# Where the experts of a strip stand in a hand-written slot plan: five slots or three

## What is computed

```python
x = x + _L0_conv_ref(_ln_c(x), ...)      # attention over routed regions, 8 heads of 8
t = t + _L0_ffn_ref(_ln_t(t), ...)       # 8 experts of 64x64, top 2
x = x + _L1_conv_ref(_ln_c(x), kernel)   # 3x3 convolution, binarized weights
t = t + _L1_ffn_ref(_ln_t(t), ...)       # 8 experts of 64x128, top 2
```

```python
for e in range(E):
    h = gelu(tokens @ w1[e] + b1[e]); y = h @ w2[e] + b2[e]
    out = out + combine[:, e:e + 1] * y
```

## Time and profile before

| | us |
|---|---|
| median of 3 runs | 6992.14 (6990.91 to 6999.84) |
| the profiled execution's own span | 6996.9 |
| VectorE busy | 6258.5 (89%) |
| TensorE busy | 5469.8 (78%) |
| GpSimd busy | 4062.8 (58%) |
| ScalarE busy | 3507.3 (50%) |

### The profile page before, as it was taken

One profiled execution on the slowest core, in us unless ns is written; L12 is line 12 of the kernel. 1 busy time (PEld: TensorE's weight loads), 2 busy tenths in 40 slices (PEclk: granted clock), 3 DMA queues, 4 the chain that ended last, 5 costly groups with the idle time before them and its releaser, 6 DMA issues. The chain is left out here.

```text
span 6996.9 us, 144425 instructions
## 1 busy us (share of the span) xinstructions
PE 5469.8 (78%) x30242; PEld 4119.1 (59%) x30242; DVE 6258.5 (89%) x25629; ACT 3507.3 (50%) x7250; POOL 4062.8 (58%) x2812
## 2 busy tenths in 40 slices
PE   4777788887878777887878787878878787777777
PEld 2665566565656565665656565656656565656654
DVE  3999999999989999999989999998999999999941
ACT  1344455555545455555545555554545555555543
POOL 2555656565656566565656566565656566656542
PEclk9667777777777787777777777777767777777777
DMA  2111111111111111111111111111111111111100
GB/s 56 28 30 33 29 29 32 30 33 31 33 30 33 27 33 29 32 31 30 33 30 33 27 34 29 35 28 30 33 30 33 30 30 26 28 27 28 30 15 13
DMA packets 501061, 212.34 MB, mean 30 GB/s; under 512 B 339456, under 2 KB 495744, under 8 KB 500096
## 3 DMA queue, kind: packets, MB, share of 16 engines
q1 hardware_dynamic: 500096, 201.91, 12.8%
HBM read 145.29 MB, written 56.37 MB: 29 GB/s over the span
## 5 line engine op out<-in xcount | busy, mean ns | idle before, releaser
L515 POOL TENSOR_SCALAR b_r<-b_r 128x1024 f32<-128x1024 f32 x392 | 1089.2, 2778 | 1491.1 <-DVE b_r L472 1483.2
L472 DVE MATCH_REPLACE8 b_r<-b_v,b_r 128x256 f32<-128x256 f32 x4704 | 1871.2, 409 | 0.0
L467 DVE MAX8 b_v<-b_r 128x8 f32<-128x256 f32 x4704 | 1641.8, 411 | 0.0
L805 POOL TENSOR_TENSOR c_h<-c_h,c_cb 128x448 f32<-128x448 f32 x672 | 762.9, 1136 | 1083.0 <-ACT c_cb L782 1061.1
L536 PE MATMUL pT_ps<-k_ident,b_e 128*128 128x128 f32 x3136 | 644.7, 343 | 603.2 <-ACT b_pT L544 589.5
L536 PEld LDWEIGHTS pT_ps<-k_ident,b_e 128*128 128x128 f32 x3136 | 489.5, 181 | 885.7 <-issue 849.5
L438 PE MATMUL s_ps<-b_kv,b_qe 128*128 128x128 f32 x6272 | 970.5, 321 | 22.1 <-POOL b_qe L424 22.1
L438 PEld LDWEIGHTS s_ps<-b_kv,b_qe 128*128 128x128 f32 x6272 | 962.3, 242 | 22.9 <-issue 22.9
L558 PEld LDWEIGHTS o_ps<-b_kv,b_pT 128*128 128x128 f32 x6272 | 872.5, 221 | 168.8 <-issue 168.5
L558 PE MATMUL o_ps<-b_kv,b_pT 128*128 128x17 f32 x6272 | 883.8, 285 | 107.5 <-ACT b_at L585 97.5
L522 POOL TENSOR_TENSOR b_e<-b_e,b_r 128x1024 f32<-128x1024 f32 x392 | 923.3, 2355 | 38.1 <-ACT b_e L508 37.8
(11 more groups left out here) (147 smaller groups left out, 8548.8 us busy)
## 6 DMA issues: line engine op xcount, KB each, us to landing
b_kv<-kv_d SPq DMA_DIRECT2D x1568, 33.0 KB, 2.0
b_q<-q_d SPq DMA_DIRECT2D x784, 16.0 KB, 1.9
c_win<-vpad_d SPq DMA_DIRECT2D x56, 145.0 KB, 2.8
c_hm<-cpad_d SPq DMA_DIRECT2D x56, 145.0 KB, 2.3
kv_d<-a_v SPq DMA_DIRECT2D x56, 119.0 KB, 2.6
vpad_d<-a_vT SPq DMA_DIRECT2D x56, 116.0 KB, 2.3
c_win<-vpad_d SPq DMA_DIRECT2D x56, 116.0 KB, 2.7
c_row<-vpad_d SPq DMA_DIRECT2D x56, 116.0 KB, 2.5
```

What stands on the lines that cost most here:

```text
L467: dve.max(out=b_v8[p][:, t, 8 * rnd:8 * rnd + 8], in_=src[:, t, :]).then_inc(chain, 1)
L472: last = dve.match_replace(out=b_r[p][:, t, :], in_to_replace=b_v8[p][:, t, 8 * rnd:8 * rnd + 8], in_values=src[:, t, :], imm_value=GONE)
L515: pool.tensor_scalar(out=b_r[p][:, :, :], in0=b_r[p][:, :, :], scalar1=GONE, scalar2=None, op0=ALU.is_le).then_inc(b_msk, 1)
L805: pool.tensor_tensor(out=D["h"][g % 2][:, :], in0=D["h"][g % 2][:, :], in1=D["cb"][g % 2][:, :], op=ALU.mult).then_inc(S["hc"], 1)
```

## The change

The experts of a strip stand in other slots. Layer 0's four, which were at 91 and 92 (two each), are all at 91. Layer 1's eight, which were at 115, 116 and 117 (three, three, two), are at 115 and 116 (four each). Modulo 7 that is slot 0 instead of 0 and 1, and slots 3 and 4 instead of 3, 4 and 5. Inside a slot the first expert's places stay; the fourth gets places of its own, and the down-projections of the second, third and fourth stand at 0.62, 0.66 and 0.68.

```diff
-        for layer, slot, gs in ((0, 91, (0, 1)), (0, 92, (2, 3)), (1, 115, (0, 1, 2)), (1, 116, (3, 4, 5)), (1, 117, (6, 7))):
-            for g, up, down, act_up, pool_up in zip(gs, (0.1, 0.32, 0.5), (0.45, 0.62, 0.64), (0.15, 0.35, 0.5), (0.25, 0.45, 0.55)):
+        for layer, slot, gs in ((0, 91, range(4)), (1, 115, range(4)), (1, 116, range(4, 8))):
+            for g, up, down, act_up, pool_up in zip(gs, (0.1, 0.32, 0.5, 0.64), (0.45, 0.62, 0.66, 0.68), (0.15, 0.35, 0.5, 0.65), (0.25, 0.45, 0.55, 0.6)):
                 PLACES["pe"][f"c{layer}", UP + g] = slot + up
                 PLACES["pe"][f"c{layer}", DOWN + g] = slot + down
                 PLACES["act"][f"c{layer}", UP + g] = slot + act_up
                 PLACES["pool"][f"c{layer}", UP + g] = slot + pool_up
```

## The result

The changed kernel takes 7081.8 us in the median of four executions (7076.2 to 7095.0), the kernel before 6995.2 in four beside them (6990.9 to 6999.8): ratio 1.0126, 95% interval 1.0106 to 1.0146, or 87 us more. The forecast was 7122, with a range of 6965 to 7235: the sign and the range held, and the size was half as large again as measured (130 for 87 us).

A forecast was written before the change was run, and what follows sets the result against it. VectorE's order, with its waits and blocked instructions, was taken to bound the kernel. Slot 2 +40, slots 3 to 6 +108 and the tail -18 made +130 us on 6992: 7122 us, range 6965 to 7235.

The forecast's parts named there:

- What bounds the kernel: Whole kernel: everything goes by VectorE's order; only what makes VectorE wait or holds up its instructions moves the end.
- Table loads: ScalarE: exp/GELU switches fall from ten loads a strip to six, 5.1 us less, counting only in slot 1.
- Stage a's walk in slot 0: Slot 0, TensorE: added experts start stage a 7.6 us later at the low clock, 5.2 at the high.
- c_p: Slots 0 and 1, ScalarE: c_p, which VectorE waits for, comes 3.9 us later in a low-clock strip.
- Saving 2.1 us: Slot 2, VectorE's steps behind c_p: less blocking by POOL saves 2.1 us, between 0.5 and 4.
- 28 x 1.8 - 12 x 0.8: Slot 2's sum: 28 low-clock strips lose 1.8 us each, 12 high-clock ones win 0.8, together +40 us.
- only a size: Clock rising in slot 0 through denser work: with all strips like the 12, the sum is +58, 7050 us.
- The copy and the exp come 2.4 us later: Slots 3 to 6: the fourth expert delays region 4's exp, then slot 6's mask; +2.2 us a strip, +108 us.
- Rival 1: TensorE's delay from slots 0 and 1 carried into slot 3: 108 becomes 206, 7220 us; chance 0.22.
- Rival 2: Slot 6: L896 is issued before the late mask, costing 0.2 us instead of 4.9; 6949 us; chance 0.17.
- The tail: After the last selection: one joint of about 2.0 us fewer per layer's group in several strips, -18 us.
- Slot 1: The gap behind slot 1's selection: forecast unchanged, 0 us.

The follow-up runs named there:

- the deferred order: VectorE's small steps of stages a, t, c0, c1 issued inside the next selection: 6824.7 us on the kernel before, 6863.6 on the changed one.
- routing earlier: The changed kernel with stage t's matmul and copy ahead of the fourth up-projection in slot 3: 7128.8 us, ratio 1.0198.
- the three with 32 matmuls: 32 matmuls with unused results added ahead of the transposes' second half in slots 0 and 7: before 6893.2 us, layer 0 gathered 6898.5, changed kernel 7044.1.
- layer 1 alone: The kernel before with only layer 1's eight experts gathered, four each in slots 3 and 4: ratio 1.0069.
- layer 0 alone: The kernel before with only layer 0's four experts gathered in slot 0: 7127.4 us, ratio 1.0194.
- layer 0 and 16 matmuls: Only layer 0's experts gathered, plus 16 unused matmuls ahead of the transposes' second half in slots 0 and 7: 7060 us, ratio 1.0097.

## Why the prediction was right in sign and wrong in size

- *What bounds the kernel.* Right as an account: selections unchanged, every difference in VectorE's gaps. That VectorE's order by itself sets the time is too strong: the deferred order took 2.8 us a strip where it would have taken 8 to 12, and slot 6's gap ends where a chain through the other engines ends (below).
- *Table loads.* Right in number: 5.8 a strip. What they are worth by themselves no run shows, since none changes them alone; that ScalarE's 264 us did not shorten the kernel is all that is measured.
- *Stage a's walk in slot 0.* Right: forecast 5.2 us later at the high clock and 7.6 at the low one, measured 4.8 (12.7 to 17.5 behind the selection's end) and 7.5 (15.6 to 23.1). So was the cause, slot 0's new wait for the fourth product, in the timeline of TensorE in after:

```profile
2731.85 0.91 PE L728 MATMUL y_ps<-k_w,c_h 128*112 128x64 f32 x8
2734.28 0.97 PE L728 MATMUL y_ps<-k_w,c_h 128*112 128x64 f32 x8 [1.52 <-POOL c_h L805]
2735.08 0.55 PE L262 MATMUL a_ps<-k_ident,a_xn 112*64 112x112 f32 x4
```

- *c_p.* Right: forecast +1.1 (5.2 less 4.1) and +3.9 us behind slot 0's selection, measured +1.2 (30.1 to 31.3) and +4.5 (32.9 to 37.4). The wait for it between 1000 and 5620 us grew from 131.1 to 151.5 us.
- *"Saving 2.1 us", VectorE's steps behind c_p.* This step failed first. I gave the steps behind c_p an even chance to be caught by the next product, and read the saving from one low-clock strip. (The sum had the two losses exchanged, too: by rows 4 L886 lost 2.3 us and L901 2.0; and 1.4 and an even chance of 2.3 make 2.6, not 2.1.) Measured 4.5 us (9.6 to 5.1), past the upper end of 4: neither is caught, since mask and spread run while VectorE still waits for c_p, and the next product waits for an exp that starts 4.5 us after c_p's end (2753.06), behind stage a's copies on ScalarE, where it was 2.4 us in before. With it a high-clock strip wins 3.9 us in slot 2 (13.3 to 9.4), forecast 0.8; a low-clock one loses 0.2 (16.1 to 16.3), forecast 1.8.
- *"28 x 1.8 - 12 x 0.8".* The second failure, larger than the first: the two counts were kept from before (28 and 12, by the values' matmuls 26 and 13). After the change 5 strips were low-clock ones. With before's 13 and 26 strips slot 2 would have given 13 x -3.9 + 26 x 0.2 = -46 us; measured -191, so some -145 are the clock's. Over the whole strips: with before's counts the change would have cost 13 x 2.3 + 26 x 5.5 = 173 us, and it cost 57 (39 x 1.5). I had named the clock "only a size"; it was a size of more than the change itself.
- *"The copy and the exp come 2.4 us later", slots 3 to 6.* The third, on the other side, and here the chain was right and a term was missing. Measured 2.1 + 1.8 + 1.9 us, forecast 2.2 for all: +231 us over 40 strips, where the term had 88. The chain is the forecast's. In each of eight kernels (before, after, either layer alone, routing earlier, and the three with 32 matmuls) the mean time from region 4's exp to slot 6's mask is 29.5 to 29.9 us, and from that mask to the next selection 9.73 to 9.76 us. The gaps of slots 4 and 5 together are 4.8 to 8.7 us in them, so VectorE's stalls there are swallowed, as forecast: without them slot 6's gap would be the longer. What was wrong is when the exp comes: 6.1 us later behind slot 3's selection, not 2.4. With layer 1 alone it is 2.6 us, and the next selection 2.2 us later, the forecast's very term. The other 3.9 us are layer 0's: the exp of region 3 already starts 2.6 us behind its selection's end where it started 0.3, since VectorE comes out of slot 2 4.3 us earlier and TensorE and ScalarE are not as much earlier: counted from slot 0's selection, region 4's exp is 1.8 us later than before. The term had this lag at nothing, and so what slot 2 wins is lost again in slots 4 to 6.
- *Rival 1*, TensorE's lag carried from slots 0 and 1 into slots 3 and on, had 0.22 and is what that term lacked: layer 0 alone lengthens slots 4 and 6 by 3.9 us a strip. Its price of 98 us was too low (40 x 3.9 = 156), and it was set against the forecast's own slot 2 gain, though both came together: in that kernel's high-clock strips slot 2 wins 4.0 us and the strip 0.6.
- *Rival 2* did not happen in its terms. Beside stage a, L896 is caught in every strip. In five of the late strips without stage a it is not (0.17 us), but there L886, six instructions ahead of it, is caught in its place, and the gap of slot 6 is 11.7 us there (14.8 in the one with the loop turn), where the nine such strips of before have 11.2 to 14.2. The instruction was the wrong thing to price; what is caught is VectorE, by the first instruction that can be. VectorE's timeline in such a strip of after:

```profile
5970.91 4.78 DVE L886 CAST c_pf<-c_pi 112x32 f32<-112x32 uint32 x1
...
5976.71 0.17 DVE L896 TENSOR_SCALAR c_z<-c_z 112x4 f32<-112x4 f32 x1
```

- *The tail*: forecast -18, measured -10. *Slot 1* (+0.6 us a strip) and the ten strips without stage a (+39 us, 36 of them slot 5, forecast 20 or so) were undersized.

The terms against each other: slot 2 came out 231 us below its term, slots 4 to 6 and the later strips 162 above theirs, slot 1 and the ends 35 above. The forecast's nearness to the result is the luck of that: two errors, each larger than the forecast itself or the result, with opposite signs.

At one clock the change costs 151 us, which is above the forecast. So the reasoning about slots undersized the harm, and the clock hid 64 us of it. What makes the clock rise in slot 0 of after and of layer 1 alone (34 and 35 strips) and not of layer 0 alone (6) is not settled. The length of the idle time ahead of the second half does not tell: in before it is 7.2 us in the mean of the high-clock strips and of the low-clock ones; 5.8 us go with a rise in after, and 3.4 us with none in layer 0 and 16 matmuls. Shown is only that with the 32 matmuls, which leave 0.6 to 3.9 us of it, the clock is high in 111 of 117 strips.

## What to carry to other kernels

- Fewer switches and fewer, fuller slots save time only on an engine that is waited for. Look at where the last of the gathered steps ends, and at what is queued behind it on every engine: here stage a, the routing copy and GpSimd's next product.
- On an engine that blocks another's instructions, the order of both around a hand-over matters more than the work: the same 0.2 us instruction took 4.8 us or 0.2. Write down for every small step what GpSimd runs at that time, at the new times.
- Where an engine's granted clock differs between repetitions of the same work, as TensorE's did in slot 0 (0.50 or 0.66 in before), two versions can differ by whole per cent for that alone: 3.3% in the kernel with layer 0 gathered. Sort the repetitions by the clock and compare like with like before pricing an edit; and try the edit with the clock held. Compare only repetitions that are alike otherwise: the deferred kernels' two halves of a loop turn were not.
- A gap in the busiest engine's timeline need not be closed by what stands in it. Follow one instruction that ends it back through the other engines, in several kernels: the interval that stays the same in all of them (here 39.2 to 39.7 us, from region 4's exp to the next selection) is the chain.

## What was not expected of the hardware

- Idle time of TensorE in the middle of slot 0 is not free: 32 unneeded matmuls (5.4 us at the high clock), in time that it waited anyway, took 6992 to 6893 us, 1.5%. By the Trainium skill (TensorE: Matmul & The Clock Gate, "HAM oscillation — how this bites in real kernels") a wait between bursts of matmuls can put the clock back to its lower level, and the cure there is to leave no such wait. The trace agrees: the four transposes behind that wait take 1.08 or 1.09 us in all 39 strips of before, of after and of layer 0 alone, and 0.63 in most strips of before where the 32 matmuls fill most of the wait; the granted clocks above are 0.50 to 0.66 and 0.79.
- The price of a low clock is not fixed: 2.3 us a strip in before, 5.5 to 5.9 with layer 0 in one slot (and 8.2 in three strips with the 32 matmuls). These kernels have more of TensorE's matmuls in slot 0, ahead of what the others wait for, which would explain it; no run varied that alone.
- A blocked VectorE instruction waits through three GpSimd instructions in a row (2462.26 to 2467.04 above: mask, spread, product), and not only for the one that ran when it was issued.
